# A four-layer transformer on one core: layer 0's modulation in the queue of common work, and a first piece's products ahead of the second piece's transposes

## The reference

```python
x = L0_attn_x_seq
mod = (_silu(L0_c) @ L0_wmod).reshape(L0_c.shape[0], 6, 1, -1)
sa, ca, ga, sb, cb, gb = (mod[:, 0], mod[:, 1], mod[:, 2], mod[:, 3], mod[:, 4], mod[:, 5])
ga = (2 * (ga >= 0) - 1) * jnp.maximum(jnp.abs(ga), 0.25)
gb = (2 * (gb >= 0) - 1) * jnp.maximum(jnp.abs(gb), 0.25)
h = _layernorm(x, axis=-1) * (1 + ca) + sa
x = x + ga * _L0_attn_ref(h, L0_attn_Wq, L0_attn_bq, L0_attn_Wk, L0_attn_bk, L0_attn_Wv, L0_attn_bv, L0_attn_gamma)
h = _layernorm(x, axis=-1) * (1 + cb) + sb
x = x + gb * _L0_ffn_ref(h, L0_ffn_w_router, L0_ffn_w1, L0_ffn_w2, L0_ffn_w3)
...
```

## Time and profile before

| | us |
|---|---|
| median of 3 runs | 1863.14 |
| lowest and highest | 1861.32, 1865.4 |
| the profiled execution | 1864.32 |
| its span in the profile | 1862.5 |
| busy: matrix engine | 1774.7 (95%) |
| busy: VectorE, ScalarE, GpSimd | 1240.2 (67%), 1099.1 (59%), 1272.5 (68%) |

### The profile page before, as it was taken

How to read it: one execution, slowest core, us unless ns; L and a number is a source line. 1 busy time by engine, 2 the same in 40 slices (tenths; PEclk the granted TensorE clock), 3 DMA queues, 4 the chain that set the end, 5 groups by cost and what they waited for, 6 DMA issues and landing times.

```text
span 1862.5 us, 31841 instructions
## 1 busy us (share of the span) xinstructions
PE 1774.7 (95%) x10270; PEld 1341.8 (72%) x10270; DVE 1240.2 (67%) x4307; ACT 1099.1 (59%) x2694; POOL 1272.5 (68%) x1779
## 2 busy tenths in 40 slices
PE   6999999989999999999999999999999999999988
PEld 4789888755676566656666576777788887788874
DVE  6853434687878877888888765434476755678674
ACT  5552324656777677767876885355345565544456
POOL 5564658999889988888988994251366755444457
PEclk8999999999999999999999999999999999999999
DMA  6100000010000000000000000000000010000002
GB/s 237 70 7 1 13 1 2 2 48 1 1 1 1 1 1 1 1 1 1 1 1 1 5 5 6 1 6 1 2 4 2 2 30 15 20 1 1 1 7 63
DMA packets 24473, 26.44 MB, mean 14 GB/s; under 512 B 3492, under 2 KB 21284, under 8 KB 23924
## 3 DMA queue, kind: packets, MB, share of 16 engines
q1 hardware_dynamic: 24308, 24.41, 4.1%
HBM read 22.26 MB, written 2.15 MB: 13 GB/s over the span
## 4 chain that ended last, share of the span: by engine, by line
PE 71%; POOL 13%; DVE 7%; issue 4%; ACT 4%; DMA 0%; POOLq 0%; SPq 0%; DVEq 0%; ACTq 0%
PE ps L86 65%; POOL arena L103 12%; PE ps L89 6%; ACT arena L97 3%; DVE arena L103 2%; DVE arena L106 1%; POOL arena L106 1%; DVE arena L126 1%; DVE arena L109 1%; DVE arena L141 1%; DVE arena L123 0%; ACT L97 0%; DVE arena L129 0%; DMA wmod<-in_wmod 0%; ACT arena L98 0%
## 5 line engine op out<-in xcount | busy, mean ns | idle before, releaser
L103 POOL TENSOR_TENSOR arena<-arena 128x128 f32<-128x128 f32 (+6 forms) x796 | 733.7, 936 | 299.8 <-DVE arena L103 105.7
L97 ACT ACTIVATE arena<-ps 128x128 f32<-128x128 f32 (+11 forms) x1100 | 364.1, 368 | 473.9 <-PE ps L86 344.3
L86 PE MATMUL ps<-arena 128*128 128x128 f32 (+4 forms) x2864 | 463.8, 296 | 18.2 <-DVE arena L103 9.8
L86 PEld LDWEIGHTS ps<-arena 128*128 128x128 f32 x2864 | 380.8, 192 | 115.3 <-issue 49.8
L103 DVE TENSOR_TENSOR arena<-ps,arena 128x128 f32<-128x128 f32 (+4 forms) x680 | 294.5, 446 | 215.3 <-PE ps L86 185.2
L97 ACT ACTIVATE arena<-arena 128x128 f32<-128x128 f32 (+1 forms) x772 | 297.2, 441 | 43.3 <-POOL arena L103 35.9
L97 ACT ACTIVATE arena<-ps,cols 128x512 f32<-128x512 f32 x324 | 217.2, 688 | 155.1 <-PE ps L86 145.0
L86 PE MATMUL ps<-arena,cst 128*128 128x360 f32 (+1 forms) x768 | 295.4, 495 | 9.6 <-POOL arena L103 6.4
L86 PE MATMUL ps<-arena,moe 128*128 128x256 f32 (+1 forms) x960 | 289.7, 442 | 0.9 <-ACT arena L97 0.8
L89 PE MATMUL ps<-cst,arena 128*128 128x128 f32 (+1 forms) x1392 | 241.3, 277 | 27.9 <-ACT arena L97 13.5
L103 POOL TENSOR_TENSOR arena<-arena,cst 128x144 f32<-128x144 f32 (+7 forms) x320 | 139.5, 439 | 142.9 <-ACT arena L97 90.2
(11 more groups left out here) (109 smaller groups left out, 1906.3 us busy)
## 6 DMA issues: line engine op xcount, KB each, us to landing
rows<-in_rows SPq DMA_DIRECT2D x1, 2253.0 KB, 14.1
arena<-in_x SPq DMA_DIRECT2D x8, 256.0 KB, 5.3
wf<-in_wf SPq DMA_DIRECT2D x2, 1024.0 KB, 6.1
arena<-in_L_ffn_W SPq DMA_DIRECT2D x8, 256.0 KB, 3.6
out_dram<-arena SPq DMA_DIRECT2D x8, 256.0 KB, 2.5
wmod<-in_wmod SPq DMA_DIRECT2D x4, 384.0 KB, 7.3
arena<-kept SPq DMA_DIRECT2D x24, 64.0 KB, 3.0
arena<-kept SPq DMA_DIRECT2D x8, 192.0 KB, 3.0
```

The source lines that it names most:

```text
L86: return UNSENT if self.e is None else self.e.matmul(out, lhsT, rhs, start=start, stop=stop)
L97: return self.e.activation(out, in_, func, bias=bias, scale=scale)
L103: return UNSENT if self.e is None else self.e.tensor_tensor(out, a, c, op)
```

## The change

Two edits are made in the text of the generators, and the tables of turns are replaced.

Layer 0's modulation moves from element 0's generators into the common ones, on ScalarE, VectorE and GpSimd (on the matrix engine it stays at the head of element 0's); its instructions count on the common semaphores now. In `common_act` it stands behind the SiLU and ahead of the decay's sigmoid, in `common_dve` between the two pairs of scans, in `common_pool` behind the first memset.

In `l0_pe` the transposes of the second piece (`turned(1)`) come behind the q and k products of the first piece, and in `l0_act` the first piece's modulated copy comes right behind its transposes, then the second piece's normalisation, the first piece's two Relus, and then the second piece's modulated copy.

All four tables in `TURNS` are new, from their first digits to the end.

```diff
--- before.py
+++ after.py
@@ -378,109 +378,109 @@
 TURNS = {
-    "pe": ("0000011001000411012001010021023101012022002101210201021100100322222101102324101330202132200131033231"
...
+    "pe": ("0123440000000100011000111000111230002111200022110032013000111220001123300103221100133231112223332221"
...
@@ -664,7 +664,7 @@
             ins.then_inc(*pe.up(b, "modT", l))
             yield
 
-        def mods_act(b, l):
+        def mods_act(b, l, s):
             for h in range(2):
                 yield
                 if l and h == 0:
@@ -673,10 +673,10 @@
                 ps = banks.get(b, "mod", l, h)
                 act.wait_ge(*at("mod", l, h))
                 act.act(mods[0:4, 384 * h:384 * h + 384], ps[0:4, 0:384]).then_inc(
-                    *act.up(b, "modrow", l, h, free=(b, "mod", l, h)))
-            yield
-
-        def mods_dve(b, l):
+                    *act.up(s, "modrow", l, h, free=(b, "mod", l, h)))
+            yield
+
+        def mods_dve(b, l, s):
             g = mods[0:4, :].rearrange("p (h i n) -> p h i n", i=3, n=128)[:, :, 2, :]
             sg = sgn[0:4, :].rearrange("p (h n) -> p h n", n=128)
             yield
@@ -684,34 +684,34 @@
                 dve.wait_ge(*at("gates", l - 1))
             dve.wait_ge(*at("modrow", l, 0))
             dve.wait_ge(*at("modrow", l, 1))
-            dve.ts(sg, g, 0.0, 2.0, ALU.is_ge, ALU.mult).then_inc(*dve.up(b))
-            yield
-            dve.wait_ge(*dve.last(b))
-            dve.ts(sg, sg, -1.0, None, ALU.add).then_inc(*dve.up(b))
-            dve.stt(g, g, -1.0, g, ALU.mult, ALU.max).then_inc(*dve.up(b))
-            yield
-            dve.wait_ge(*dve.last(b))
-            dve.stt(g, g, 0.25, sg, ALU.max, ALU.mult).then_inc(*dve.up(b, "gates", l))
+            dve.ts(sg, g, 0.0, 2.0, ALU.is_ge, ALU.mult).then_inc(*dve.up(s))
+            yield
+            dve.wait_ge(*dve.last(s))
+            dve.ts(sg, sg, -1.0, None, ALU.add).then_inc(*dve.up(s))
+            dve.stt(g, g, -1.0, g, ALU.mult, ALU.max).then_inc(*dve.up(s))
+            yield
+            dve.wait_ge(*dve.last(s))
+            dve.stt(g, g, 0.25, sg, ALU.max, ALU.mult).then_inc(*dve.up(s, "gates", l))
             yield
             ps = banks.get(b, "modT", l)
             dve.wait_ge(*at("modT", l))
-            dve.cp(mcols[:, 24 * l:24 * l + 24], ps[:, 0:24]).then_inc(*dve.up(b, "mcols", l, free=(b, "modT", l)))
-            yield
-
-        def mods_pool(b, l):
+            dve.cp(mcols[:, 24 * l:24 * l + 24], ps[:, 0:24]).then_inc(*dve.up(s, "mcols", l, free=(b, "modT", l)))
+            yield
+
+        def mods_pool(b, l, s):
             c = mods[0:4, :].rearrange("p (h i n) -> p h i n", i=3, n=128)[:, :, 1, :]
             yield
             pool.wait_ge(*at("modrow", l, 0))
             pool.wait_ge(*at("modrow", l, 1))
-            pool.ts(c, c, 1.0, None, ALU.add).then_inc(*pool.up(b, "shift", l))
+            pool.ts(c, c, 1.0, None, ALU.add).then_inc(*pool.up(s, "shift", l))
             yield
 
 
 
         def l0_pe(b):
             m = L0Attn(room[b])
-            for g in range(2):
-                yield
+
+            def turned(g):
                 ps = banks.take(pe, b, b, "l0x", g)
                 pe.wait_ge(*arrives("ident"))
                 pe.wait_ge(*at("l0n_act", b, g))
@@ -720,7 +720,9 @@
                 for i in range(4):
                     ins = pe.tr(ps[:, col4(i)], m.xn[:, col4(i)], ident)
                 ins.then_inc(*pe.up(b, "l0x", b, g))
-                yield
+
+            yield
+            turned(0)
             for g in range(2):
                 hg = m.hT[:, 512 * g:512 * g + 512]
                 yield
@@ -732,6 +734,9 @@
                 ps = banks.take(pe, b, b, "l0k", g)
                 pe.mm(ps[:, :], w0[:, 128:256], hg).then_inc(*pe.up(b, "l0k", b, g))
                 yield
+                if g == 0:
+                    turned(1)
+                    yield
                 for i in range(4):
                     yield
                     t = 4 * g + i
@@ -760,19 +765,25 @@
         def l0_act(b):
             yield
             m, r = L0Attn(room[b]), room[b]
-            for g in range(2):
+            def normed(g):
                 act.wait_ge(*at("l0stats", b, g))
                 if g:
                     act.wait_ge(*at("l0x", b, g - 1))
                 for t in range(4 * g, 4 * g + 4 - g):
                     norm_act(b, m.xn[:, col4(t % 4)], r.x[:, t, :], t, "l0n_act", b, g)
-                yield
+
+            def shifted(g):
                 ps = banks.get(b, "l0x", g)
                 act.wait_ge(*at("l0x", b, g))
                 act.wait_ge(*at("mcols", 0))
                 act.act(m.hT[:, 512 * g:512 * g + 512], ps[:, :], scale=mcol(0, 1, b), bias=mcol(0, 0, b)
                         ).then_inc(*act.up(b, "l0h", b, g, free=(b, "l0x", g)))
-                yield
+
+            normed(0)
+            yield
+            shifted(0)
+            yield
+            normed(1)
             for g in range(2):
                 yield
                 if g:
@@ -788,6 +799,9 @@
                 act.act(m.kT, ps[:, :], ACT.Relu, bias=col("bk0")).then_inc(
                     *act.up(b, "l0kT", b, g, free=(b, "l0k", g)))
                 yield
+                if g == 0:
+                    shifted(1)
+                    yield
             leave(act, b, "l0")
 
         def l0_dve(b):
@@ -2641,7 +2655,7 @@
         def common_act():
             act.wait_ge(*arrives("ct"))
             act.act(sil[:, :], ct[:, :], ACT.Silu).then_inc(*act.up(COMMON, "sil"))
-            yield
+            yield from mods_act(0, 0, COMMON)
             act.wait_ge(*arrives("rows0"))
             act.act(gd[:, 1:2], row("decay", 0, 1), ACT.Sigmoid).then_inc(*act.up(COMMON, "decay"))
             yield
@@ -2661,6 +2675,7 @@
             for dst, g in ((dec0, gd[:, 0:1]), (dec2, gd[:, 1:2])):
                 gs = g.broadcast_to([128, 128])
                 if dst is dec2:
+                    yield from mods_dve(0, 0, COMMON)
                     dve.wait_ge(*at("decay"))
                 dve.scan(dst[:, 0:128], gs, ident, 0.0, ALU.mult, ALU.add).then_inc(*dve.up(COMMON))
                 dve.scan(dst[:, 128:256], gs, gs, 1.0, ALU.mult, ALU.bypass).then_inc(
@@ -2685,7 +2700,7 @@
 
         def common_pool():
             pool.memset(mhalf[:, :], -0.5).then_inc(*pool.up(COMMON, "mhalf"))
-            yield
+            yield from mods_pool(0, 0, COMMON)
             pool.wait_ge(*arrives("cst"))
             pool.wait_ge(*arrives("rows"))
             pool.cp(three, row("bqkv", 0, 1536)).then_inc(*pool.up(COMMON))
@@ -2719,11 +2734,9 @@
             yield from l3f_pe(b)
 
         def element_act(b):
-            if b == 0:
-                yield from mods_act(b, 0)
             yield from l0_act(b)
             if b:
-                yield from mods_act(b, b)
+                yield from mods_act(b, b, b)
             yield from moe0_act(b)
             yield from l1_act(b)
             yield from moe1_act(b)
@@ -2733,11 +2746,9 @@
             yield from l3f_act(b)
 
         def element_dve(b):
-            if b == 0:
-                yield from mods_dve(b, 0)
             yield from l0_dve(b)
             if b:
-                yield from mods_dve(b, b)
+                yield from mods_dve(b, b, b)
             yield from moe0_dve(b)
             if b == 0:
                 yield from fold_dve(b)
@@ -2749,11 +2760,9 @@
             yield from l3f_dve(b)
 
         def element_pool(b):
-            if b == 0:
-                yield from mods_pool(b, 0)
             yield from l0_pool(b)
             if b:
-                yield from mods_pool(b, b)
+                yield from mods_pool(b, b, b)
             yield from moe0_pool(b)
             yield from l1_pool(b)
             yield from moe1_pool(b)
```

204 lines of the change are left out of this document (102 added, 102 removed).

## The result

| | before | after |
|---|---|---|
| median, us | 1863.02 (20 runs) | 1858.94 (20 runs) |
| lowest and highest | 1861.13, 1865.4 | 1855.71, 1862.86 |
| the profiled execution | 1864.32 | 1858.92 |
| its span | 1862.5 | 1857.1 |
| matrix engine busy | 1774.7 | 1768.9 |

The ratio is 0.9979, 95% interval 0.9972 to 0.9986: 4.1 us less. The forecast was 1858.9. The number is right; the parts that add up to it are not, as the trace and the experiments show.

The account below looks back on a forecast made before the run. The matrix engine was taken to bound most of the run, queue order the beginning. A 7.4 us lead less 3.2 given back, with 0 for the rest, made 4.2 us less: 1860.1 profiled, median 1858.9, range 1852 to 1870.

Parts of the forecast that it names:

- lead at the first state step: Beginning of layer 0: VectorE's first state step at about 20.5 us instead of 27.91, 7.4 us earlier, 8 at most.
- idle time of the matrix engine up to 30 us: Sign of being right, at the beginning: this idle time gets smaller by some 7 us.
- The moved table load: ScalarE, beginning: the sigmoid with its load, 1.28 us, stands behind the normalisations and is hidden by the wait for transposes.
- VectorE gives back 3.2 us: Layer 0 before the first expert product: four more state steps, 7.6 us of VectorE work, take 3.2 us of the lead.
- its better case: Layer 0: the four more state steps fit into VectorE's 6.4 us of idle time and cost nothing.
- The first expert product: Sign on the matrix engine: at no more than 76.4 - 4.2 us plus some 6 us of moved matrix work.
- The rival in which it stays low: Layer 0's state steps at half clock for another 4 us of matrix work: 1862; two no-change cases 0.29 together.
- The rest of the new order, 0: The long stretch after the beginning: same work in another order, taken as 0 us with 8 us to either side.
- what is gained before 100 us is kept to 400: Matrix engine, 100 to 400 us: busy 296.7 of 300 us, so earlier work is kept to 400 us at least.
- layer 1 starts late: Start of layer 1 on GpSimd: 13 more expert instructions ahead, 16.5 us; 1875, or 1867 if half hidden; chance 0.25.
- 7.4 - 3.2 + 0 = 4.2: Whole program: lead less what VectorE gives back, nothing for the rest; 4.2 us less, median 1858.9 us.
- The range of 8 us either way for the rest: Long stretch: 8 us to either side of 0, a quarter of the matrix engine's 30.9 us idle from 400 to 1100 us.

Follow-up runs that it names:

- the switches at 250 and 400 us: Changed kernel with its own order up to 250 or 400 us of its trace, behind that the order of the kernel before: 1854.05 and 1863.57 us.
- the one at 550 us: Changed kernel with its own order up to 550 us of its trace, behind that the order of the kernel before: 1878.95 us.
- the earlier switch: Changed kernel with its own order up to 120 us of its trace, behind that the order of the kernel before: 1853.48 us.

## Why the prediction was right in its number and wrong in its sum

1. **The beginning.** Right in mechanism and order; undersized. Forecast lead at the first state step 7.4, "8 at most", measured 8.7; idle time of the matrix engine up to 30 us smaller by 6.8, forecast "some 7". The inputs landed sooner than the profile page's median of 5.3 us after their issue: the first half was there at 4.62, 3.4 us after its issue at 1.18 in this trace as well; the second half was used 4.0 us after its issue at 2.66; the median is over eight, most of them issued later. The moved table load was hidden, as said: 10.55 to 11.83, and ScalarE waited 0.59 us for the transposes behind it. What the steps left out is that the normalisation stands behind both copies of the modulation on ScalarE.
2. **"VectorE gives back 3.2 us": the step that failed first.** It gave back little or nothing. The lead was 8.4 at 40 us and 10.1 at 100; 1.7 of the growth is the fall of the clock that the trace before has at 77 us and this one hasn't, which leaves 8.4 at both. From 50 to 100 us VectorE was busy for 43.8 us and the matrix engine waited for it less than before: 2.7 us from 40 to 100 us, against 4.2. The four further state steps fitted into its idle time in full, which the prediction had as its better case. I had taken "a little under half" between two bounds with no row behind it. The first expert product came at 73.73 us, 2.7 earlier, although more work stands ahead of it.
3. **The clock.** The rival in which it stays low didn't come in this trace. The first products still run at half speed (four 128x512 records take 3.6 us to the next row, against 1.8 from 19.03), to about 18 us. Then no row shows a fall until 330 us, where the trace before has them near 80 and 135, at 1.7 us of busy time each. That is 3.4 us by 140 us that wasn't in the forecast, but it is no property of the new order: the traces of the switches at 250 and 400 us, the same order up to there, have a fall at 86 and at 71 us, and the one at 550 us has falls at 71 and 88. From 30 us to the end the trace after loses as much as that of before (9.5 against 9.3 us).
4. **"The rest of the new order, 0": the step that failed second.** The prediction put the term at nothing, with 8 us to either side and no row for its middle. It costs about 5 us (1858.94 against 1854.05, and against 1853.48 with the earlier switch), most of it between 300 and 600 us by waits and idle time. With it fell the sentence that what is gained before 100 us is kept to 400: from 100 to 400 us the matrix engine was busy for 293.3 us instead of 296.7, and the lead went from 13.4 at 300 us to 8.5 at 400. This is the place of the rival "layer 1 starts late", at a third of its price. GpSimd's idle time did grow there, by 6.5 us, but it wasn't the only one that the matrix engine waited for: its products waited 4.8 us more for VectorE and 2.9 more for GpSimd. How the waits arise from single turns stays open.
5. **The sum.** Forecast 7.4 - 3.2 + 0 = 4.2. By the runs: some 9 for the beginning with the old rest, 5 lost in the rest, 4.1 left. Two errors of 5 us each cancelled, so that the number came out to the tenth is luck. The range of 8 us either way for the rest was what the prediction had right about its own ignorance.

A rule of the Trainium skill stood against the change (page "TensorE: Matmul & The Clock Gate", section "HAM oscillation — how this bites in real kernels": waits that are longer than the bursts between them bring the half clock back again and again). The half clock of the beginning ended near 18 us and came back nowhere in layer 0 in the trace after, but that hardly tries the rule: from 20 to 100 us no wait of the matrix engine is longer than 0.8 us. The falls at 71 and 86 us in other executions of this order came with waits just as short.

What beats both kernels is the changed kernel with the old order from 120 us on: 1853.48 us, 0.9950 of before, and that with a table nobody made for it. A table planned for the new beginning alone, keeping the old starts of layer 1, is the next thing to try; that it gains more isn't shown.

## What to carry to other kernels

Ask which work stands in the shadow of a wait it doesn't need: sixteen statistics that depended on nothing in the modulation stood behind it, and moving them was worth about 6 us in each of two orders. When an edit comes with a new order for the whole program, they are two changes: run the new beginning with the old order behind it before believing that the edit was small. And a hybrid of two orders is evidence only where it gains; where it loses, look at the seam first. And before a fall of the clock is put down to an edit, look whether another execution of the same order has it too.

## What the runs showed of the hardware

**The granted clock isn't shown before its first event.** The profile after gives 1.00 from the start, yet the products at 13.47 are spaced as at half clock:

```profile
13.47 3.78 PE L86 MATMUL ps<-arena,w 128*128 128x512 f32 x4 [0.87 <-ACT arena L97]
...
19.03 1.93 PE L86 MATMUL ps<-arena,w 128*128 128x512 f32 x4
```

Same form, same count, twice the time. At the start of a trace the spacing of equal records tells the clock, not the column.

**A fall of the clock needs no pause around it.** In the kernel before it came with the matrix engine busy for 7.99 of 8 us (and for 2.70 of the 4 us before these):

```profile
74.00:78.00 4.00, 3.99 (x26) 3.50 (x27) 3.19 (x24) 2.85 (x4) 1.16 (x3) 0.90 0.01 2
78.00:82.00 4.00, 4.00 (x20) 3.63 (x19) 1.80 (x20) 0.36 (x1) 0.00 (x0) 0.68 0.01 4
```

In the kernel after one stands behind a wait of 1.9 us for GpSimd:

```profile
330.00:335.00 5.00, 3.18 (x6) 1.97 (x7) 1.06 (x3) 2.22 (x4) 5.00 (x4) 0.72 0.00 0
335.00:337.50 2.50, 2.50 (x11) 1.77 (x10) 1.95 (x4) 0.31 (x1) 2.34 (x3) 0.88 0.00 0
```

A fall shows as 0.83 in a slice of 10 us, 1.7 us withheld. From 30 us on the traces here have from three to some ten of them, for the same work.

**Falls differ between executions of one order.** The two rows from 80 to 90 us in the experiments show it: the same order and the same busy time of 9.76 us, once at 0.83 and once at 1.00. The twenty executions of the changed kernel have mean granted clocks from 0.989 to 0.997 and times from 1855.71 to 1862.86. What sets a fall off where no long pause stands before it stays open.
